# Two attention exchanges of a graph kernel: 800 targets and two heads a step, and another form of the scores

## What is computed

```python
e = jax.nn.leaky_relu(s_src[src] + s_tgt[tgt], 0.2)
exp_e = jnp.exp(e - jnp.max(e))
denom = jax.ops.segment_sum(exp_e, tgt, num_segments=n)
attn = exp_e / (denom[tgt] + 1e-16)
agg = jax.ops.segment_sum(proj[src] * attn[:, :, None], tgt, num_segments=n)
```

## Time and profile before

| what | us |
|---|---|
| median of three runs | 8230.14 (8227.47 to 8231.27) |
| span of the profiled execution, first to last instruction | 8222.6 |
| what lies around the span, by the median run | 7.5 |
| adjacency stage | about 60 to 776 |
| four-head exchange | about 1790 to 2590 |
| two-head exchange | about 7680 to 8090 |

### The profile page before, as it was taken

How to read it: one execution, slowest core, us unless ns; L and a number is a source line. 1 busy time by engine, 2 the same in 40 slices (tenths; PEclk the granted TensorE clock), 3 DMA queues, 4 the chain that set the end, 5 groups by cost and what they waited for, 6 DMA issues and landing times. The chain is left out here.

```text
span 8222.6 us, 89523 instructions
## 1 busy us (share of the span) xinstructions
PE 4441.3 (54%) x17662; PEld 2239.8 (27%) x17663; DVE 4305.0 (52%) x6914; ACT 1771.4 (22%) x3075; POOL 2614.6 (32%) x2742
## 2 busy tenths in 40 slices
PE   4665673317775255276655666555665444430474
PEld 2333572102222122263222333222332222210121
DVE  6654573989997599226322333123332111227895
ACT  1343111115553322134200111001110000010352
POOL 0000002200000000100477775777776777740000
PEclk7887786669997577698767787667886666665797
DMA  1245563323332355314556666556665555553453
GB/s 37 98 145 171 203 238 132 115 87 90 91 90 83 130 213 221 111 59 170 182 163 180 201 204 194 157 172 193 201 205 162 159 160 161 162 148 113 134 140 115
DMA packets 545943, 1230.98 MB, mean 150 GB/s; under 512 B 75384, under 2 KB 371934, under 8 KB 525730
## 3 DMA queue, kind: packets, MB, share of 16 engines
q0 software_dynamic: 174992, 568.57, 23.8%
q1 hardware_dynamic: 353394, 572.26, 21.0%
q10 hardware_dynamic: 17488, 89.38, 2.8%
HBM read 968.38 MB, written 261.55 MB: 150 GB/s over the span
## 5 line engine op out<-in xcount | busy, mean ns | idle before, releaser
L2261 POOL DMA_INDIRECT rel1s_rows<-rel_table,rel1s_at x848 | 813.5, 959 | 309.5 <-issue 221.2
L2261 POOL DMA_INDIRECT rel0s_rows<-rel_table,rel0s_at x848 | 813.4, 959 | 286.3 <-issue 221.8
L2261 POOL DMA_INDIRECT rel2s_rows<-rel_table,rel2s_at x848 | 802.7, 947 | 290.1 <-issue 209.6
L2356 PE MATMUL rel2s_acc<-rel2s_rows,rel2s_hot 128*128 x848 | 465.3, 559 | 573.2 <-SPq L2249 552.0
L1403 PE MATMUL gatx_acc<-gatx_w,gatx_feat 128*65 128x400 f32 x1600 | 581.2, 506 | 229.4 <-DVE gatx_w L1326 229.4
L2356 PE MATMUL rel0s_acc<-rel0s_rows,rel0s_hot 128*128 x848 | 409.6, 495 | 457.5 <-SPq L2249 448.4
L2356 PE MATMUL rel1s_acc<-rel1s_rows,rel1s_hot 128*128 x848 | 411.3, 497 | 451.6 <-SPq L2249 438.6
L1669 POOL DMA_INDIRECT mixa_y<-y_sorted,g_rank x25 | 23.7, 950 | 1794.0 <-PEq L75 1786.6
L1363 ACT ACTIVATE gatx_w<-gatx_w,gatx_s 128x400 f32<-128x400 f32 x800 | 437.1, 617 | 329.7 <-DVE gatx_w L1317 325.8
L1317 DVE SCALAR_TENSOR_TENSOR gatx_w<-gatx_t,gatx_s 128x400 f32 (+1 forms) x800 | 453.9, 632 | 1.2 <-ACT gatx_t L1357 1.2
L1403 PE MATMUL latx_acc<-latx_w,latx_feat 128*65 128x400 f32 x800 | 311.9, 513 | 121.6 <-DVE latx_w L1326 121.6
(11 more groups left out here) (515 smaller groups left out, 8245.5 us busy)
## 6 DMA issues: line engine op xcount, KB each, us to landing
mamb_bc<-dbc SPq DMA_DIRECT2D x64, 1600.0 KB, 6.6
agg_strip<-strips SPq DMA_DIRECT2D x100, 800.0 KB, 5.9
adj<-adj_counts SPq DMA_DIRECT2D x25, 1600.0 KB, 6.2
gatx_adj<-adj SPq DMA_DIRECT2D x200, 200.0 KB, 2.4
latx_adj<-adj SPq DMA_DIRECT2D x200, 200.0 KB, 2.3
rel_table<-rel0p_prod POOLq DMA_DIRECT2D x25, 1536.0 KB, 5.3
rel_table<-rel0s_prod ACTq DMA_DIRECT2D x25, 1536.0 KB, 6.3
rel_table<-rel1s_prod ACTq DMA_DIRECT2D x25, 1536.0 KB, 6.2
```

The source lines that it names most:

```text
L2261: pool.indirect_dma_start(rows[:, u, k, :], None, table, bass.IndirectOffsetOnAxis(ap=at[:, n:n + 1], axis=0)).then_inc(s_in[u], 16)
L2356: nc.tensor.matmul(acc[a][:, :], to, row[:, 0:2 * D], start=fresh and k == 0, stop=False)
```

## The change

The targets' block grows from J = 400 to J = 800, and a step treats two heads. The four-head exchange thus has four blocks of targets times two pairs of heads, 8 x 25 = 200 steps; the two-head exchange has 4 x 25 = 100 steps. A step in both has scores for two heads of 800 columns, two exponentials of 800 columns, one multiplication over 2 x 800 and, in TensorE, two heads times two halves of 400 columns. Each step loads 128 x 800 counts and the features of two heads.

In the four-head exchange the factor that depends on the target alone is taken out of the numerator and the denominator. The score becomes max(0.8 t1, -0.8 s), which needs one tensor, so its instruction is a TENSOR_SCALAR; the 1e-16 in the denominator gets the factor instead (`floor`, a tile of 128 x 100 numbers made once), and `heads_to_nodes` adds that tile where it added a constant. Two maxima instead of one are found ahead of it. t2 and the instructions that made it are gone.

Beside this, `three_of` loads two of a group's three numbers with one register load and the third by a load of its own.

```diff
-J = 400
+J = 800
...
-                    v(nc.vector.tensor_reduce(top_p[:, :], top_m[:, 0:T - 1, :], AX.XY, ALU.max))
-                    v(nc.vector.tensor_reduce(top4[0:real, 0, 0:1], top_m[0:real, T - 1, :], AX.X, ALU.max))
-                    v(nc.vector.tensor_tensor(top_p[0:real, :], top_p[0:real, :], top4[0:real, 0, 0:1], ALU.max))
+                    v(nc.vector.scalar_tensor_tensor(best[:, :, :], scores[:, :, H:2 * H], -0.2, top_m[:, :, :], ALU.mult, ALU.add))
+                    for k, tops in enumerate((top_m, best)):
+                        one = top_p[:, k:k + 1]
+                        v(nc.vector.tensor_reduce(one, tops[:, 0:T - 1, :], AX.XY, ALU.max))
+                        v(nc.vector.tensor_reduce(top4[0:real, 0, 0:1], tops[0:real, T - 1, :], AX.X, ALU.max))
+                        v(nc.vector.tensor_tensor(one[0:real, :], one[0:real, :], top4[0:real, 0, 0:1], ALU.max))
...
-            feat = [ph.sb(f"feat{u}", [P, H * 65]) for u in range(U)]
-            w = [ph.sb(f"w{u}", [P, H, J]) for u in range(U)]
+            feat = [ph.sb(f"feat{u}", [P, 2 * 65]) for u in range(U)]
+            w = [ph.sb(f"w{u}", [P, 2, J]) for u in range(U)]
...
-            acc = [[ph.ps(f"acc{k}_{h}", [65, J]) for h in range(H)] for k in range(2)]
+            acc = [[ph.ps(f"acc{k}_{h}", [65, 2, BANK]) for h in range(2)] for k in range(2)]
...
-                    sp.dma_start(allp[:, :], row(m_dram[0:1, 0:P].rearrange("o p -> (o p)"))).then_inc(s_row, 16)
+                    for k in range(2):
+                        sp.dma_start(allp[:, k, :], row(m_dram[k:k + 1, 0:P].rearrange("o p -> (o p)"))).then_inc(s_row, 16)
...
-                    sp.dma_start(feat[u][:, :], pr_dram[bass.ds(a, P), 0:H * 65]).then_inc(s_in[u], 16)
+                    sp.dma_start(feat[u][:, :], pr_dram[bass.ds(a, P), hp * 130:(hp + 1) * 130]).then_inc(s_in[u], 16)
...
-                    v(nc.vector.tensor_reduce(allm[:, :], allp[:, :], AX.X, ALU.max))
-                    v(nc.vector.tensor_scalar(t2[:, H // 2:, :], t1[:, H // 2:, :], 0.2, None, ALU.mult))
-                    v(nc.vector.tensor_scalar(s02[:, :, :], scores[:, :, 0:H], 0.2, allm[:, 0:1], ALU.mult, ALU.subtract))
+                    v(nc.vector.tensor_reduce(allm[:, :], allp[:, :, :], AX.X, ALU.max))
+                    v(nc.vector.tensor_scalar(bias[:, :, :], scores[:, :, 0:H], allm[:, 1:2], None, ALU.subtract))
+                    v(nc.vector.tensor_tensor(allm[:, 0:1], allm[:, 0:1], allm[:, 1:2], ALU.subtract))
+                    v(nc.vector.tensor_scalar(floor[:, :, :], scores[:, :, H:2 * H], -0.2, allm[:, 0:1], ALU.mult, ALU.add))
+                    v(nc.vector.tensor_scalar(floor[:, :, :], floor[:, :, :], 85.0, -50.0, ALU.min, ALU.max))
...
-                    for h in range(H):
-                        last = nc.vector.scalar_tensor_tensor(w[u][:, h, :], t1[:, h, bass.ds(c, J)],
-                                                              s08[:, bass.ds(s, 1), h], t2[:, h, bass.ds(c, J)],
-                                                              ALU.add, ALU.max)
+                    for h in range(2):
+                        to, row_h, s_h = w[u][:, h, :], t1[:, 2 * hp + h, bass.ds(c, J)], s08[:, bass.ds(s, 1), 2 * hp + h]
+                        if by_target:
+                            last = nc.vector.scalar_tensor_tensor(to, row_h, s_h, t2[:, 2 * hp + h, bass.ds(c, J)], ALU.add, ALU.max)
+                        else:
+                            last = nc.vector.tensor_scalar(to, row_h, 0.8, s_h, ALU.mult, ALU.max)
...
-                    for h in range(H):
-                        last = nc.scalar.activation(w[u][:, h, :], w[u][:, h, :], ACT.Exp, bias=s02[:, bass.ds(s, 1), h])
+                    for h in range(2):
+                        last = nc.scalar.activation(w[u][:, h, :], w[u][:, h, :], ACT.Exp, bias=bias[:, bass.ds(s, 1), 2 * hp + h])
...
-                        for h in range(H):
-                            last = nc.tensor.matmul(acc[k][h][:, :], feat[u][:, h * 65:(h + 1) * 65], w[u][:, h, :], start=False, stop=False)
+                        for h, a in halves:
+                            last = nc.tensor.matmul(acc[k][h][:, a, 0:J // 2], feat[u][:, h * 65:(h + 1) * 65],
+                                                    w[u][:, h, a * (J // 2):(a + 1) * (J // 2)], start=False, stop=False)
...
-                nc.vector.tensor_scalar(den[:, :].unsqueeze(2), heads[:, :, 64:65], floor[1], None, floor[0]).then_inc(s_v, 1)
+                if floor is None:
+                    least = nc.vector.tensor_scalar(den[:, :].unsqueeze(2), heads[:, :, 64:65], 1e-30, None, ALU.max)
+                else:
+                    least = nc.vector.tensor_tensor(den[:, :].unsqueeze(2), heads[:, :, 64:65],
+                                                    floor[:, bass.ds(t, 1), :].rearrange("p a h -> p h a"), ALU.add)
...
-    eng.reg_load(regs, table[0:1, bass.ds(n, 1), :].rearrange("o n k -> o (n k)"))
+    eng.reg_load(regs[:2], table[0:1, bass.ds(n, 1), 0:2].rearrange("o n k -> o (n k)"))
+    before = eng.value_load(table[0:1, bass.ds(n, 1), 2], min_val=0, max_val=last)
     why = "made by edge_tables within these bounds"
-    first, count, before = (eng.snap(r) for r in regs)
+    first, count = (eng.snap(r) for r in regs[:2])
```

More of the change, by code:

```diff
@@ L1246, in attention, with place, columns, rounds @@
             s_z, s_e, s_w, s_used, s_sum, s_out, s_st = ph.sems("z", "e", "w", "used", "sum", "out", "st")
-            s_mp, s_t2 = ph.sems("mp", "t2")
+            s_mp, s_low = ph.sems("mp", "low")
             R = T // U
             block = ph.block()
-            def rounds(eng, step, j, some):
-                def one(i):
+            def place(i, k):
+                return (2 * i + k, 0) if HP == 1 else (i, k)
+            def columns(eng, i, k):
+                j, hp = place(i, k)
+                return (j * J if isinstance(j, int) else eng.snap(j * J)), hp
+            def rounds(eng, step, i, k, some):
+                b = 2 * i + k
+                def one(r):
                     for u in range(U):
-                        step(j, i * U + u, j * T + i * U + u, j * R + i, u)
+                        step(i, k, r * U + u, b * T + r * U + u, b * R + r, u)
                 if len(some) == 1:
                     return one(some[0])
[L1260 to L1265, removed]
+                with eng.Fori(some[0], some[-1] + 1, 1) as r:
+                    one(r)
             @block.sync
@@ L1269, in _ @@
                 if not by_target:
-                    with nc.allow_non_contiguous_dma(reason="one number for each partition"):
-                        sp.dma_start(m_dram[0:1, 0:P].rearrange("o p -> p o"), top_p[:, :]).then_inc(s_mp, 16)
+                    with nc.allow_non_contiguous_dma(reason="two numbers for each partition"):
+                        sp.dma_start(m_dram[0:2, 0:P].rearrange("o p -> p o"), top_p[:, :]).then_inc(s_mp, 16)
                 sp.dma_start(t1[:, :, :].rearrange("p h n -> p (h n)"),
@@ L1364, in step, with others, end @@
                     last.then_inc(s_e, 1)
-                def end(j, k):
-                    act.wait_ge(s_sum, j + 1)
-                    act.wait_ge(s_st, j * 16)
-                    for h in range(H):
-                        last = nc.scalar.copy(agg[:, h, :], acc[k][h][:, :])
+                def others(i, k):
+                    rounds(act, step, i, k, range(1, R))
+                def end(i, k):
+                    b = 2 * i + k
+                    act.wait_ge(s_sum, b + 1)
+                    act.wait_ge(s_st, b * 16)
+                    for h in range(2):
+                        last = nc.scalar.copy(agg[:, h, :].rearrange("c (a n) -> c a n", a=2), acc[k][h][:, :, 0:J // 2])
@@ L1371, in end @@
                     last.then_inc(s_out, 1)
[L1372 removed]
+                    act.wait_ge(s_out, b + 3)
                     act.sem_inc(g.waited, 1)
[L1374 to L1385 removed]
@@ L1386, in _ @@
-                rounds(act, step, NJ - 2, others)
-                rounds(act, step, NJ - 1, first)
-                end(NJ - 2, 0)
-                rounds(act, step, NJ - 1, others)
-                end(NJ - 1, 1)
-                act.wait_ge(s_st, NJ * 16)
+                    at, hp = columns(act, i, k)
+                    act.dma_start(agg_dram[2 * hp:2 * hp + 2, :, bass.ds(at, J)].rearrange("h c n -> c h n"),
+                                  agg[:, :, :]).then_inc(s_st, 16)
+                first = range(1)
@@ new lines, in _ @@
+                rounds(act, step, 0, 0, first)
+                with act.Fori(0, NB // 2 - 1, 1) as i:
+                    for k in range(2):
+                        others(i, k)
+                        rounds(act, step, i + k, 1 - k, first)
+                        end(i, k)
+                others(NB // 2 - 1, 0)
+                rounds(act, step, NB // 2 - 1, 1, first)
+                end(NB // 2 - 1, 0)
+                others(NB // 2 - 1, 1)
```

(3 more changed lines are left out.)

120 lines of the change are left out of this document (61 added, 59 removed).

## The result

| | before | changed |
|---|---|---|
| median, us | 8229.9 (8227.5 to 8231.3, 4 runs) | 8086.9 (8075.0 to 8089.1, 4 runs) |
| ratio | | 0.9826 (95%: 0.9812 to 0.9840) |
| profiled span, us | 8222.6 | 8073.0 |

The changed kernel is 1.7% faster. The forecast was 8081, in a range of 8035 to 8140. The profiled execution of the changed kernel took 8075.0, the shortest of the four (the other three 8086 to 8089), so its span is some 12 us short of the median; of what follows, differences inside a stage are firmer than the span's.

A forecast was written before the change was run, and what follows sets the result against it. VectorE was taken to bound both exchanges and its sequencer the adjacency stage. Span 8222.6 - 218 (four-head) - 30 (two-head) - 1 (preparation) + 100 (register loads) + 7.5 = 8081 us, range 8035 to 8140.

The forecast's parts named there:

- rival 1: Whole kernel: the forecast itself, a four-head step of 2.83 us and a second load of about 0.5: 8081 us, chance 0.64.
- four-head steps: Four-head exchange: a step of 2.83 us instead of 3.92, 200 times: -218 us, bounds -244 to -184.
- two-head steps, with their end: Two-head exchange: 100 steps of 3.66 us, 366 instead of 399.4, plus a longer last step, copy and store: -30 us.
- preparation: Ahead of the four-head exchange: t2's work goes, small VectorE instructions and about 1 us idle come: -1 us (-4 to +2).
- guards of the denominator: The 25 guards change their kind and not their size: 0 to +1 us, taken as 0.
- register loads: Adjacency stage: a second load in each of 200 groups, +0.51 us a group on VectorE: +100 us, bounds +15 and +130.
- around the span: Whole kernel: 7.5 us added to the profiled span of 8222.6 to reach the median of the runs, 8230.1.
- Rival 5: Four-head scores: the one-tensor score runs at one element a cycle, a step of 3.66 us, +166, 8247 us; chance 0.04.
- Rival 3: Four-head exchange: TensorE or the ring sets the step at 3.0 us, +34, 8115 us; chance 0.10.
- Rival 6: Four-head exchange: TensorE's clock falls to half speed, 5.4 us a step, +514, 8595 us; chance 0.03.
- rival 2: Adjacency stage: the second load is hidden or nearly free, +15 in place of +100, 7996 us; chance 0.10.
- the 190 waits for "issue": Adjacency stage: VectorE's waits for its own sequencer, 217.0 us before, were to grow by the second load's whole added time.

The follow-up runs named there:

- steps of 400: The changed kernel with J = 400 in both exchanges, the one-tensor form of the four-head scores kept: 8171.6 us, ratio 0.9937.
- one head weighted: The changed kernel with only the first of a step's two heads multiplied by the counts, in both exchanges: 7976.4 us, ratio 0.9698.
- The kernel without the check: The changed kernel with two register loads, but a register maximum in place of the bounds check on the third number: 8044.9 us, ratio 0.9774.
- one load again: The changed kernel with the three words in one register load and a register maximum in place of the bounds check: 7998.5 us, ratio 0.9721.

## Why the prediction was right

The forecast's mechanism, rival 1, is what happened. By its own steps:

| term | predicted | measured |
|---|---|---|
| four-head steps | -218 | -218.6 (784.1 to 565.5) |
| two-head steps, with their end | -30 | -29.8 |
| preparation | -1 | about -2 (-3.0 from load to first score, +1.0 ahead of it) |
| guards of the denominator | 0 | +2.9 |
| register loads | +100 | +91.6 in the trace; +97 alone in the kernel before |
| parts that the change does not touch | 0 | +6.2 (2.7, 1.3 and 2.2 in three places) |
| around the span | 7.5 | 2.0 in the profiled run |

Without the last row they add up to -150, as the spans do (-149.6); the forecast's terms add up to -149. That the two agree to 1 us is partly luck: the register loads came 8 us below their price, and the guards and the untouched parts 9 us above theirs. Why the untouched parts grew is open.

**The four-head step** was priced at 2 x 0.546 + 1.74 and came at 2.83. The single score lasts 624 ns for 633 predicted; the timeline's 1.17 us for two has the overlap in it. The kernels with two-tensor scores and with steps of 400 separate its two causes: at 800 columns the form saves 3.66 - 2.83 = 0.83 us a step (166 us), and the larger block with the old form 3.92 - 3.66 = 0.26 (52 us), sum 218. The 66 us of the kernel with steps of 400 are not the same quantity, since there the multiplication is halved too. In the scores alone the block saves no more with the new form than with the old: two of 400 columns exceed one of 800 by 2 x 409 - 624 = 194 ns with one tensor, and by 2 x 632 - 1033 = 231 with two; the halved multiplication adds 2 x 973 - 1811 = 135 for each step. Rival 5 (8247) would have been right only if a TENSOR_SCALAR ran at the two-tensor pace; the kernel that puts the second tensor back, a step of 3.66, came at 8251.

**TensorE** was said to keep up with little to spare, 2.7 against 2.83. The run with one head weighted shows its own pace, 2.73, so the margin was 0.10 us a step, 20 us over the exchange. Rival 3's 3.0 us, with a start-up of TensorE in every step, did not come: VectorE's steps stayed at 2.83. The expected idle time near 0.1 us a step is there, but in the rows of the weight loads and not in those of the products. The lag that the prediction counted on exists only in the first seven steps of a block (thirteen in the first block); after them TensorE waits for the weights of each step, and VectorE never waits for it. Rival 6 did not come: the granted clock of the window is 0.99.

**DMA** is busy at a share of 0.60 with 169 GB/s; 168 and about 0.63 were forecast. No wait of VectorE inside the steps names a load.

**The register loads.** +0.46 us a group of one chunk, where +0.51 was priced. The groups with more chunks, which were to cover a little of it, grew as much (0.45 and 0.44 us of idle time on average). The loads came as priced: 527 and 294 ns for 0.53 and 0.30. One item was left out: the register instruction behind the loads shrank from 107 to 54 ns, having one value less to treat. The kernel without the check shows that the price has two nearly equal halves, 46 us for a load that has its own fixed part and its own register instruction, and 42 for the check beyond a maximum (some 11). So rival 2 (7996) fails twice: one load again measures 7998, that is, the gain that the split gave away. One statement of the prediction was wrong: that the 190 waits for "issue" would grow by the whole. They fell to 136, and those for TensorE rose from 33 to 86 (40.5 to 119.6 us). Both sequencers carry the second load; that TensorE's groups then start late more often, and VectorE waits behind the ring of two slots, is my reading. In 127 of the 200 groups the head still waits for "issue". TensorE's passes also became slower, with the granted clock at 0.78 in place of 0.84, and no run holds that clock fixed, so a part of the 92 us may come through it. Either way the split is what sets it off, since one load again takes it back: 88 us, and a granted clock of 0.85. Whether one of the two sequencers alone would give the whole cost wasn't tried.

By the Trainium skill, "Runtime: NRT & Kernel Launch", Instruction fetch mechanics, a register costs about 200 ns even in bulk; the rows come near it (294 ns for one word, 527 for two, 759 for three: 0.23 for each further one). The page speaks of the launch's own loads from HBM, while this table lies in a tile on the core. The floor of about 600 ns in "DMA: Bandwidth & Descriptors", Latency and other measured facts, does not hold for these loads (294 and 527 ns), and the sum by it, 8140, was 53 too high.

**The preparation** had one idle microsecond too many: ScalarE's table load stands ahead of the data (it ran at 1858.92), so nothing delayed the first weights. Of the seven small instructions behind the load there are six, and they take 2.25 us up to the first score, for 2.1 estimated. The **guards** were taken at 0 and cost 0.12 us each. The two rows are one guard of before and one after:

```profile
2596.54 0.16 DVE L1460 TENSOR_SCALAR loch_den<-loch_tp 128x4 f32<-128x4 f32 x1 [0.79 <-PE loch_tp L1451]
```

```profile
2470.67 0.16 DVE L1495 TENSOR_TENSOR loch_den<-loch_tp,loc_floor 128x4 f32<-128x4 f32 x1 [0.92 <-PE loch_tp L1483]
```

The instruction lasts 0.16 us in both; it starts 0.13 later behind the transpose that it waits for. The new one takes a slice of `floor` whose place depends on the loop's counter; that the address is worked out in that time is my reading, and no run tested it.

**Around the span** the profiled run has 2.0 us in the changed kernel and 1.9 to 2.8 in the experiments, and 2.1 in the runs of the kernel before that stand beside them. The 7.5 of the forecast, and the statement ahead of it that the profiled execution took its span and 7.5 us, were the distance from one profiled span to the median of other runs: some 2 us around the span, and for the rest the spread between runs. With 2 us the forecast would have been 8076, still in its range, and 11 us below the median in place of 6. That it came this close is luck here too.

## What to carry to other kernels

Ask of each short loop whether any engine fills it; if none does, price the sequencer's register work at its full duration, word by word: here a split load with a bounds check gave back 90 of 250 us, and one packed word with a running sum in a register (7926) beats both kernels. An instruction with one tensor source and one scalar took half the time an element of one with two tensor sources, so an algebraic step that removes a source is worth more than merging instructions (166 us against 52), and larger instructions, which pay the fixed part less often, come after it. When a bound falls, compare the new step with the next engine's own pace: here it stood at 2.73 of 2.83, so further work on VectorE's side of the four-head exchange buys 20 us and no more. The rows of TensorE's products looked full at that point; its weight loads showed the pauses.

## What the runs showed of the hardware

The slowest register loads scale with the words too, and four times as steeply: 999 ns for one word, 1923 for two, 2799 for three by the maxima above, about 0.9 us a word where a usual further word costs 0.23. In the traces with three words in one load such a load stands at about every eighth of the 200 groups, 24 times in all, with a milder one some three groups ahead of most; with fewer words more loads are hit (over two and a half times the median: 24 with three words, 52 with two, 65 with one). Eight groups are one strip of the matrix, and SP's stores of the finished strip run at these moments; that the loads wait behind the stores is argued from that timing alone. By size it fits the gain from two words to one: the time by which VectorE's slower loads exceed the median sums to 65 us with two words and to 43 with one, 22 us, beside the 10 of the plain groups. But with three words that sum is 60, no more than with two, and the granted clock rose from 0.84 to 0.91 at the same time, so this explanation is not shown.
